# Moving the rotary products, the causal mask and part of a scale-and-shift between engines in a fused attention and feed-forward layer

## What is computed

```python
xn = _layernorm(x, axis=-1)
s = _L0_attn_ref(xn, L0_attn_W_in, L0_attn_W_out)
g = _silu(_L0_ffn_ref(xn, L0_ffn_w1, L0_ffn_b1, L0_ffn_ln_g, L0_ffn_ln_b, L0_ffn_w2, L0_ffn_b2))
x = x + s * g
```

```python
scores = jnp.einsum('bhqd,bhkd->bhqk', q, k) * scale
scores = jnp.where(causal[None, None], scores, jnp.finfo(scores.dtype).min)
attn = jax.nn.softmax(scores, axis=-1)
out = jnp.einsum('bhqk,bhkd->bhqd', attn, v)
```

```python
h = jax.nn.silu(bitlinear158(x, w1, b1))
h = jax.nn.gelu(h, approximate=False)
h = layer_norm(h, ln_g, ln_b)
return bitlinear158(h, w2, b2)
```

## Time and profile before

| what | value |
|---|---|
| timed, median of 2 runs | 8135.92 us (8042.31 and 8229.52) |
| the profiled execution | 7962.75 us |
| its span, slowest core (core 4) | 7961.2 us |
| spans of the 8 cores | 7878.7 to 7961.2 us |
| busy share on core 4 | PE 53%, DVE 30%, ACT 20%, POOL 13% |

### The profile page before, as it was taken

One profiled execution on the slowest core, in us unless ns is written; L12 is line 12 of the kernel. 1 busy time (PEld: TensorE's weight loads), 2 busy tenths in 40 slices (PEclk: granted clock), 3 DMA queues, 4 the chain that ended last, 5 costly groups with the idle time before them and its releaser, 6 DMA issues.

```text
span 7961.2 us, 51095 instructions; the slowest of 8 cores (7878.7 to 7961.2 us)
## 1 busy us (share of the span) xinstructions
PE 4236.5 (53%) x18688; PEld 1825.9 (23%) x18688; DVE 2403.2 (30%) x2459; ACT 1612.2 (20%) x1427; POOL 1049.3 (13%) x590
## 2 busy tenths in 40 slices
PE   1157566623446777788677279700000013965956
PEld 0123222201112222333233134200000001422423
DVE  5513344454552000344345201122222331011011
ACT  1100000022335555111111200033333331000000
POOL 0000000000110000011222100033444332000000
PEclk9998788856678888799888689755555556987978
DMA  2111222265782000666577731022222224677766
GB/s 80 56 53 37 58 65 66 62 242 197 216 232 79 22 20 19 193 221 203 181 223 245 241 98 56 27 69 76 82 63 63 63 63 106 146 181 178 145 174 148
DMA packets 380349, 945.65 MB, mean 119 GB/s; under 512 B 49860, under 2 KB 279364, under 8 KB 347076
## 3 DMA queue, kind: packets, MB, share of 16 engines
q1 hardware_dynamic: 315528, 707.47, 31.3%
q0 software_dynamic: 64576, 234.92, 9.8%
HBM read 707.44 MB, written 234.88 MB: 118 GB/s over the span
## 4 chain that ended last, share of the span: by engine, by line
PE 43%; DMA 19%; DVE 15%; ACT 8%; issue 4%; POOLq 4%; POOL 4%; ACTq 2%; DVEq 1%; SPq 1%; another core or an unknown queue 0%
PE pM L1298 11%; PE pF L901 6%; PE pO L979 6%; DMA wstg<-wkvq 4%; DMA w1b<-w1t_sc 4%; POOLq L1104 4%; POOL ab L1105 4%; DMA qbuf<-q_sc 3%; PE pA L665 3%; PE pB L665 3%; DMA h_sc<-hsil 3%; PE pAV L781 2%; PE pA L555 2%; DMA y<-ocb 2%; PE pB L555 2%
## 5 line engine op out<-in xcount | busy, mean ns | idle before, releaser
L901 PE MATMUL pF<-w1b,xq1b 128*128 128x512 bf16 x4096 | 927.5, 390 | 296.0 <-DMA w1b<-w1t_sc 244.3
L1298 PE MATMUL pM<-x2q,w2b 128*128 128x512 bf16 x4096 | 901.5, 381 | 67.5 <-DMA w2b<-w2t_sc 67.5
L1160 PE MATMUL pT<-identb,xqt 128*128 128x128 bf16 x1024 | 130.3, 301 | 1365.2 <-DVE xqt L1146 1337.0
L771 ACT ACTIVATE Pp<-pS 128x1024 bf16<-128x1024 f32 x544 | 550.6, 1023 | 897.9 <-PE pS L756 533.5
L901 PEld LDWEIGHTS pF<-w1b,xq1b 128*128 128x128 bf16 x4096 | 405.9, 100 | 818.7 <-issue 367.5
L979 PE MATMUL pO<-woutb,abuf 128*128 128x512 bf16 x2048 | 444.6, 380 | 171.5 <-DMA abuf<-at_sc 171.5
L1298 PEld LDWEIGHTS pM<-x2q,w2b 128*128 128x128 bf16 x4096 | 399.9, 98 | 543.6 <-issue 78.7
L751 PE MATMUL pS<-qbuf,k_fm 128*128 128x512 bf16 x544 | 245.1, 451 | 422.2 <-DMA qbuf<-q_sc 213.2
L1160 PEld LDWEIGHTS pT<-identb,xqt 128*128 128x128 bf16 x1024 | 90.2, 128 | 1406.7 <-issue 1397.4
L665 PE MATMUL pA<-xn_fm,wres 128*128 128x512 bf16 x1024 | 234.4, 389 | 316.8 <-ACT wres L648 316.8
L912 DVE SCALAR_TENSOR_TENSOR htmp<-pF,c1c,b1bc 128x512 f32<-128x512 f32 x256 | 190.9, 750 | 622.1 <-PE pF L901 490.4
(11 more groups left out here) (171 smaller groups left out, 5058.3 us busy)
## 6 DMA issues: line engine op xcount, KB each, us to landing
wch<-w1T SPq DMA_DIRECT2D x32, 4096.0 KB
wch<-w2T SPq DMA_DIRECT2D x128, 1024.0 KB
h_sc<-hsil POOLq DMA_DIRECT2D x256, 256.0 KB, 4.3
hbF<-h_sc SPq DMA_DIRECT2D x16, 4096.0 KB
wstg<-wkvq SPq DMA_DIRECT2D x96, 512.0 KB
w1t_sc<-tern POOLq DMA_DIRECT2D x16, 2048.0 KB, 27.1
w1b<-w1t_sc SPq DMA_DIRECT2D x16, 2048.0 KB
w2t_sc<-tern POOLq DMA_DIRECT2D x64, 512.0 KB, 8.2
```

Source lines behind the costliest of these rows:

```text
L771: ev_e = b.do("scalar", lambda s, par=par: s.activation(Pp[par][:], pS[par][:], AF.Exp, scale=SC_ATT), mark="ac")
L901: ins = t.matmul(ps[:], xq1b[:, dc * T + qt * 128: dc * T + (qt + 1) * 128], wb_[:, dc * 512:(dc + 1) * 512], start=(dc == 0), stop=(dc == ...
L1298: ins = t.matmul(ps[:], wb2_[:, oc * 128:(oc + 1) * 128], x2q[:, oc * 512:(oc + 1) * 512], start=(oc == 0), stop=(oc == NOC - 1))
```

## The change

The change has three parts.

1. The rotary products (`ropek`, `ropeq`). ACT now copies the result of a unit from PSUM to bf16 tiles in SBUF in three instructions, once straight (`krawb`, `qrawb`) and twice with the halves of the partitions swapped (`krotb`, `qrotb`). DVE multiplies these by bf16 tables, with 128 partitions at a time, so it has two products and one add. PSUM is free for the next matmuls after ACT's copies. The tables and the mask are loaded as bf16.
2. The causal mask. At `kt == qt`, PE adds the mask by two more matmuls, the identity against `tri2b`, into the same PSUM accumulation. DVE's L766 is gone.
3. The gain and shift of F2. POOL works on the last 3072 of the 8192 columns and DVE on the first 5120. The maximum and the squares wait for both.

```diff
@@ P1kv, the units of k
-                            v.tensor_mul(a32[:], ps[:], cosT[:, sl])
-                            v.tensor_mul(b32[0:64, :], ps[64:128, :],
-                                         ssT[0:64, sl])
-                            v.tensor_mul(b32[64:128, :], ps[0:64, :],
-                                         ssT[64:128, sl])
+                        b.waits("scalar", [ev_mm, prev_kr])
+
+                        def evk(sc, ps=ps):
+                            sc.copy(krawb[:], ps[:])
+                            sc.copy(krotb[0:64, :], ps[64:128, :])
+                            return sc.copy(krotb[64:128, :], ps[0:64, :])
+                        ev_kc = b.do("scalar", evk, mark="ac")
+                        prev_evac[unit % 2] = ev_kc
+                        b.wait("vector", ev_kc)
...
+                            v.tensor_mul(a16[:], krawb[:], cosTb[:, sl])
+                            v.tensor_mul(b16[:], krotb[:], ssTb[:, sl])
                             v.drain()
@@ P2q, the units of q
-                    b.waits("vector", [ev_mm, st_free[unit % 2]])
+                    b.waits("scalar", [ev_mm, prev_r_any])
+
+                    def evq(sc, ps=ps):
+                        sc.copy(qrawb[:], ps[:])
+                        sc.copy(qrotb[0:64, :], ps[64:128, :])
+                        return sc.copy(qrotb[64:128, :], ps[0:64, :])
+                    ev_qc = b.do("scalar", evq, mark="ac")
+                    prev_rope[unit % 2] = ev_qc
+                    b.waits("vector", [ev_qc, st_free[unit % 2]])
@@ P3flash, the scores
+                        stp = (kt != qt)
...
+                        if kt == qt:
+                            t.matmul(pS[par][:, 0:512], identb[:],
+                                     tri2b[:, 0:512], start=False,
+                                     stop=True)
+                            ins = t.matmul(pS[par][:, 512:1024], identb[:],
+                                           tri2b[:, 512:1024], start=False,
+                                           stop=True)
+                        return ins
...
-                    if kt == qt:
-                        b.wait("vector", ev_s)
-                        ev_m = b.do("vector", lambda v, par=par:
-                                    v.tensor_tensor(pS[par][:], pS[par][:],
-                                                    tri2[:], ALU.add),
-                                    mark="dv")
-                        src_ev = ev_m
@@ F2, gain and shift
+            SPL = 5120
             b.waits("gpsimd", [ev_zn, pool_prev])
-            ev_gm = b.do("gpsimd", lambda g, ab=ab: (
-                g.tensor_mul(ab[:], ab[:], gbc[:]),
+            ev_gmp = b.do("gpsimd", lambda g, ab=ab: (
+                g.tensor_mul(ab[:, SPL:DI], ab[:, SPL:DI], gbc[:, SPL:DI]),
                 g.drain(),
-                g.tensor_add(ab[:], ab[:], bbc[:]))[-1], mark="gp")
+                g.tensor_add(ab[:, SPL:DI], ab[:, SPL:DI],
+                             bbc[:, SPL:DI]))[-1], mark="gp")
...
+            b.waits("vector", [ev_zn])
+            ev_gmv = b.do("vector", lambda v, ab=ab: (
+                v.drain(),
+                v.tensor_mul(ab[:, 0:SPL], ab[:, 0:SPL], gbc[:, 0:SPL]),
+                v.drain(),
+                v.tensor_add(ab[:, 0:SPL], ab[:, 0:SPL],
+                             bbc[:, 0:SPL]))[-1], mark="dv")
+            ev_gm = ev_gmp
+            b.waits("vector", [ev_gmp, ev_gmv])
```

More of the change, by code:

```diff
@@ L125, in build_nc @@
     b2_h = inp("b2", [1, D])
[L126 to L128 removed]
+    cosb_h = inp("cosTb", [128, T], BF16)
+    sinb_h = inp("sinTb", [128, T], BF16)
+    tri_h = inp("trimask", [128, 1024], BF16)
     id_h = inp("ident", [128, 128])
@@ L201, in build_nc @@
     er = rope_ctx.enter_context
[L202 to L205, removed]
+    cosTb = er(nc.sbuf_tensor("cosTb_sb", [128, T], BF16))
+    ssTb = er(nc.sbuf_tensor("ssTb_sb", [128, T], BF16))
+    b.dma("sync", cosTb[:], cosb_h[:, :])
+    b.dma("sync", ssTb[:], sinb_h[:, :])
     b.phase = "A"
@@ L604, in ropek @@
                                      oc * T + (tb + 1) * 1024],
-                                a32[:], b32[:])
+                                a16[:], b16[:])
                         ev_r = b.do("vector", ropek, mark="dv")
-                        prev_evac[unit % 2] = ev_r
+                        prev_kr = ev_r
                     unit += 1
@@ L754, in smm @@
                                  qb[:, kvh0 * 512:(kvh0 + 1) * 512],
[L755 to L760, removed]
+                                 start=True, stop=stp)
+                        ins = t.matmul(pS[par][:, 512:1024],
+                                       k_fm[:, kvh1 * T + kt * 128:
+                                            kvh1 * T + (kt + 1) * 128],
+                                       qb[:, kvh1 * 512:(kvh1 + 1) * 512],
+                                       start=True, stop=stp)
+                        if kt == qt:
[6 more added lines that the diff above has]
+                        return ins
                     ev_s = b.do("tensor", smm, mark="pe")
                     src_ev = ev_s
-                    if kt == qt:
-                        b.wait("vector", ev_s)
-                        ev_m = b.do("vector", lambda v, par=par:
-                                    v.tensor_tensor(pS[par][:], pS[par][:],
-                                                    tri2[:], ALU.add),
-                                    mark="dv")
-                        src_ev = ev_m
                     b.waits("scalar", [src_ev, pe_z.get(g - 2)])
@@ L1100, in build_nc @@
                              scale=C(INVc)))[-1], mark="ac")
+            SPL = 5120
             b.waits("gpsimd", [ev_zn, pool_prev])
[L1102 to L1103 removed]
+            ev_gmp = b.do("gpsimd", lambda g, ab=ab: (
+                g.tensor_mul(ab[:, SPL:DI], ab[:, SPL:DI], gbc[:, SPL:DI]),
                 g.drain(),
[L1105 to L1110 removed]
+                g.tensor_add(ab[:, SPL:DI], ab[:, SPL:DI],
+                             bbc[:, SPL:DI]))[-1], mark="gp")
+            pool_prev = ev_gmp
+            b.waits("vector", [ev_zn])
[7 more added lines that the diff above has]
+            b.waits("vector", [ev_gmp, ev_gmv])
+            ev_mx = b.do("vector", lambda v, C=C, ab=ab: (
+                v.drain(),
+                v.reduce_max(C(T2c), ab[:], AX.X,
+                             apply_absolute_value=True))[-1], mark="dv")
+            b.waits("scalar", [ev_gm, ev_gmv, sq2_prev])
             ev_sq2 = b.do("scalar", lambda s, C=C, ab=ab, xq=xq:
@@ L1409 @@
     cosT, sinT = _rope_tables()
+    cosTb = cosT.astype(ml_dtypes.bfloat16)
+    sinTb = sinT.astype(ml_dtypes.bfloat16)
     base = np.where(np.arange(128)[:, None] > np.arange(128)[None, :],
                     np.float32(-1e30), np.float32(0.0)).astype(np.float32)
-    trimask = np.ascontiguousarray(np.tile(base, (1, 8)))
+    trimask = np.ascontiguousarray(
+        np.tile(base, (1, 8)).astype(ml_dtypes.bfloat16))
     ident = np.eye(128, dtype=np.float32)
```

43 lines of the change are left out of this document (20 added, 23 removed).

## The result

The changed kernel takes 0.971 of the time of before (95% interval 0.968 to 0.974): 2.9% faster, where the forecast was 3.1%. Its profiled execution is 7700.14 us, against 7962.75 before; the forecast on that scale was 7719, and the time that was given, on the scale of 8042, was 7798. The medians of all executions are 7961.91 us (11 of them, 7699.58 to 8010.86) and 8062.94 us (10, 7920.88 to 8293.46); that of after lies 12 us above the forecast range of 7530 to 7950. Stage times are means over the cores of one profiled execution.

What follows compares the result with a forecast made beforehand. PE alone was taken to bound much of the program, with F2's unoverlapped steps, DVE in early P3flash and transfers elsewhere. 7962.75 - 173 - 77 + 11 - 5 = 7719 us, given as 8042 - 244 = 7798; range 7530 to 7950.

Steps and rivals of the forecast that it cites:

- The mechanism of F2: Gain and shift of F2: DVE and POOL take turns, 24.5 us for four instructions, 173 us gained; chance 0.52.
- side by side: Rival: DVE and POOL work at once in F2, 13.5 us a pair, 349 us gained, 7622 us in all; chance 0.34.
- The evidence for the choice, one row with L482: POOL's issue of an `at_sc` transfer took 4.12 us beside DVE's L482, 0.71 with DVE idle; taken to favour turns.
- The mask: P3flash, causal mask moved from DVE to PE: 77 us gained, between 45 and 200.
- Late pairs: P3flash, 28 pairs without thunks: the detour through DVE goes, 0.95 us gained each, 27 us.
- Early pairs: P3flash, 36 pairs with thunks: DVE's chain shortens; 50 us taken, between bounds of 18 and 177.
- The bound of 177: Upper bound for the 36 early pairs of P3flash: all gain comes through until transfers are never idle, 96 + 81 us.
- absorbed: Rival: transfers absorb the mask's early gain, P3flash gives 45 us and F2 takes turns, 7830 us; chance 0.10.
- The rotary products: P1kv and P2q: units gain nothing, first casts at quarter ends wait behind ACT's copies; 11 us lost.
- The 2 us for the two stage ends: Ends of P1kv and P2q: the last unit's 3.1 + at most 3.7 us against 4.9, counted as 2 us lost in all.
- The start: Loads ahead of the first x tile: tables and mask lose 1.25 MB, 5 us gained.
- The scale: Time given from 8042, the middle of three executions of before, minus 244: 7798 us; on the profiled execution's scale 7719.

Runs made afterwards that it cites:

- f2_reduce: Changed kernel with DVE's product and sum over 5120 columns in F2 replaced by two maxima (reduce_max): ratio to before 0.952, F2 1190.2 us.
- f2_tscalar: Changed kernel with DVE's two F2 operations on 5120 columns replaced by one-input multiply-adds by constants: ratio to before 0.961, F2 1271.0 us.
- late tiles: Kernels loading each query tile behind the w1 loads, as before: P3flash 1542 us with the mask on DVE, 1473 with it on PE (means).
- early tiles: Kernels loading the query tile one tile ahead, before the w1 loads: P3flash 1469 us with the mask on DVE, 1393 with it on PE.

## Why the prediction was right

**The mechanism of F2 was right, and its size nearly.** The forecast had 24.5 us for the four instructions, and 24.1 were measured; it had 173 us, and the stage lost 180. DVE's instruction was put at 5.49 us and takes 5.34 once it is let in, twice in a tile; 16 x 0.4 = 6.4 us is the difference. The Trainium skill, "SBUF — State Buffer", section "Who interferes with whom", states that the blocked side waits for the whole instruction, and this trace agrees (11.99 us beside 6.64). It also says that a reduction never contends on this chip; f2_reduce agrees, with 5.49 and 6.66 us side by side. And it lists `tensor_scalar` among the operations that can, and f2_tscalar agrees, with 2.68 us behind POOL's end. The rival "side by side" fell: it had 13.5 us for the pair, and f2_reduce shows that 13.84 is what it would have been. The evidence for the choice, one row with L482, was of another kind of instruction, as the prediction says; it pointed the right way, but it could not decide. That the trace of before shows nothing for two inputs is not quite so: it has L486 beside POOL's issues, 0.54 us each, which speaks for the other end and was not weighed.

**The mask was right in its sum, and for the early pairs partly by luck.** 77 us were forecast and 73 measured, 68 by the means. Late pairs: 0.95 us each against 0.93, as worked out. Early pairs: 50 against 47 (18 + 29). This 50 was picked between 18 and 177 and not worked out, so its nearness is luck. The reason that was given for a low value, that the next `qbuf` takes back what is won, holds for the sums: the wait grew by 67 us over P3flash, and the gain in the sums is 14 us with late tiles and 38 with early ones. For the ternary pieces it isn't shown; there the gain is no larger with early tiles (12 against 29). The bound of 177 took the transfers alone and was far too high: even with early tiles a pair in the sums stops at 13.0 us, the load of w1, and not at DVE's 10.2. The "absorbed" rival (45 us in all) falls too. What limits the ternary pieces of the kernel after, with late tiles, was not separated.

**The rotary products were mis-sized a little.** 11 us were forecast, 7.8 measured (9 by the mean of twelve kernels). Each quarter's first cast does start 3.07 us later, and PE's pauses at the three quarter ends grew by 2.8 us each, 8.4 in all. The 2 us for the two stage ends aren't there: DVE's products in bf16 take 0.69 us (L700 in the groups below), where up to 1.23 had been allowed. Nothing of it shows within a quarter, as forecast.

**The start** gave 3.5 us, 5 were forecast. At the rate that the prediction names, 3.6 MB in 16.52 us, 1.25 MB are 5.7 us and not 5; the 16.52 us also hold whatever doesn't depend on the bytes, which was left in. F1's -3.5 has no cause in the change; that stage came to 1362 to 1390 us in kernels that share its code.

**The scale.** The time that was given, 7798 us, starts from 8042, the middle of three executions. It lies between the profiled execution of after, 7700, and the median of all, 7962, and meets neither. What can be held against the record is the difference to before: 244 us or 3.1%, where the ratio says 2.9%.

## What to carry to other kernels

Before work is split between DVE and POOL, ask what kind of instruction DVE will run beside POOL's: with two inputs from SBUF, or of the kind that does two elements at a time, they take turns, and every column given to the slower engine (POOL 2.1 ns, DVE 1.04 here) adds its full time. Which property of the two-input kind does it was not held apart here. The split 5120 to 3072 won 180 us over POOL alone and lost 105 against DVE alone. Busy time doesn't show when one engine keeps the other out; compare the length of an instruction with that of the same one alone. And work moved off an engine that waits for PE anyway, as the rotary products, gains nothing, and costs where it puts something in front of other work: here about 8 us for the copies ahead of three casts.

## What the hardware showed that was not expected

Being kept out counts as busy: DVE's busy time rises through F2 (380 us for L1131 and L1133, of which 32 x 5.34 = 171 are work), and L1131 reads 11.99 us for 5.34 us of work. Who comes first is not settled by the start on the page: DVE's L1131 stands at 5375.25 and POOL's L1123 at 5375.26, and it was DVE that waited. A copy on ACT costs the same for 64 partitions as for 128 (1009 and 1012 ns by the groups below), so halving the partitions saves nothing.

```profile
L690 ACT CAST qrawb<-pA 128x1024 bf16<-128x1024 f32 x32 | 32.4, 1012 | 146.6 <-PE pA L676 146.6
L691 ACT CAST qrotb<-pA 64x1024 bf16<-64x1024 f32 x32 | 32.3, 1009 | 0.4
L700 DVE TENSOR_TENSOR a16q<-qrawb,cosTb_sb 128x1024 bf16<-128x1024 bf16 x64 | 44.3, 692 | 641.7 <-ACT qrotb L692 641.7
```

DVE's product of 1024 columns takes 692 ns in bf16 from SBUF, 1225 in float32 with one input in PSUM.
